# Causal mask of the second layer's first score squares: identity products on TensorE in place of VectorE's additions, with a new written-out order

## What is computed

```python
def _L1_attn_ref(x, w_qkv, w_proj, b_proj):      # B, S, dim = 8, 512, 256; 16 heads of 16
    qkv = (x @ w_qkv).reshape(B, S, 3, heads, head_dim)
    Q, K, V = (qkv[:, :, 0], qkv[:, :, 1], qkv[:, :, 2])
    Q = apply_rope(Q)
    K = apply_rope(K)
    attn = jnp.einsum('bqhd,bkhd->bhqk', Q, K) * scale
    causal = jnp.tril(jnp.ones((S, S), dtype=bool))[None, None]
    attn = jnp.where(causal, attn, jnp.asarray(NEG_INF, attn.dtype))
    attn = jax.nn.softmax(attn, axis=-1)
    out = jnp.einsum('bhqk,bkhd->bqhd', attn, V).reshape(B, S, dim)
    return out @ w_proj + b_proj
```

## Time and profile before

| | us |
|---|---|
| median of 3 runs | 1977.19 |
| lowest, highest | 1975.2, 1977.64 |
| the profiled execution | 1979.78 |
| its span, first to last instruction | 1978.0 |
| PE busy in the span | 1856.4 (94%) |
| DVE busy | 1375.4 (70%) |
| ACT, POOL busy | 907.2, 510.0 |

### The profile page before, as it was taken

The page is one execution under the profiler, slowest core; times in us unless marked ns, Lnnn a source line. Parts: engine busy times, 40 slices in busy tenths (PEclk is TensorE's granted clock), DMA queues, the critical chain, the costliest instruction groups (busy, mean ns, idle before and its releaser), DMA issues.

```text
span 1978.0 us, 39009 instructions
## 1 busy us (share of the span) xinstructions
PE 1856.4 (94%) x15449; PEld 1293.8 (65%) x15449; DVE 1375.4 (70%) x2407; ACT 907.2 (46%) x1116; POOL 510.0 (26%) x597
## 2 busy tenths in 40 slices
...
PEclk8898999999999999888999999999999999999999
...
GB/s 184 58 46 42 59 37 73 50 58 28 86 52 26 40 39 5 171 1 17 44 81 78 54 85 62 65 87 50 75 96 30 86 93 44 86 84 43 112 83 43
DMA packets 171812, 126.26 MB, mean 64 GB/s; under 512 B 113944, under 2 KB 148720, under 8 KB 171248
## 3 DMA queue, kind: packets, MB, share of 16 engines
...
q10 hardware_dynamic: 832, 0.01, 0.0%
...
## 4 chain that ended last, share of the span: by engine, by line
PE 77%; DVE 15%; ACT 4%; issue 3%; POOL 1%; DMA 0%; SPq 0%; DVEq 0%; POOLq 0%; ACTq 0%
PE ps L2041 24%; PE ps L2025 5%; PE ps L1078 5%; PE ps L1922 4%; PE ps L1984 3%; PE ps L983 3%; PE ps L1952 3%; PE ps L2055 2%; PE ps L1108 2%; PE ps L1041 2%; PE ps L1130 2%; PE ps L1023 2%; DVE b_maxima L1689 2%; PE ps L1968 2%; PE ps L1964 2%
## 5 line engine op out<-in xcount | busy, mean ns | idle before, releaser
L2041 PE MATMUL ps<-b_acts,b_hidden_w 128*128 128x512 f32 x2048 | 504.6, 398 | 1.1 <-POOL b_acts L1616 1.1
L2041 PEld LDWEIGHTS ps<-b_acts,b_hidden_w 128*128 128x128 f32 x2048 | 376.2, 188 | 90.9 <-issue 9.8
L452 POOL TENSOR_SCALAR_AFFINE_SELECT a_probs<-a_probs 128x512 f32<-128x512 f32 (+1 forms) x224 | 166.3, 758 | 357.4 <-ACT a_probs L863 249.1
L1608 POOL TENSOR_SCALAR_AFFINE_SELECT b_work<-b_work 128x512 f32<-128x512 f32 x128 | 83.3, 663 | 673.1 <-ACT b_work L1843 673.0
L1879 ACT ACTIVATE b_acts_exact<-ps,c_s 128x512 f32<-128x512 f32 x128 | 88.2, 689 | 297.6 <-PE ps L2041 297.4
L863 ACT ACTIVATE a_probs<-ps 128x2048 f32<-128x2048 f32 (+1 forms) x96 | 153.2, 1595 | 123.5 <-DVEq L713 86.7
L1843 ACT ACTIVATE b_work<-ps 128x2048 f32<-128x2048 f32 (+1 forms) x96 | 153.4, 1597 | 90.8 <-PE ps L1968 89.0
L1689 DVE TENSOR_REDUCE b_maxima<-ps 128x4 f32<-128x2048 f32 (+3 forms) x128 | 187.9, 1489 | 3.3
L1787 DVE CAST b_acts<-b_acts_exact 128x512 fp32r<-128x512 f32 x128 | 55.8, 436 | 164.2 <-ACT b_acts_exact L1879 163.9
L1078 PE MATMUL ps<-a_probs,c_va 128*17 128x192 f32 (+4 forms) x2048 | 136.6, 388 | 2.9 <-issue 1.5
L1686 DVE TENSOR_TENSOR ps<-ps,c_causalr 128x512 f32<-128x512 f32 x128 | 86.1, 696 | 45.2 <-PE ps L1952 43.4
...
## 6 DMA issues: line engine op xcount, KB each, us to landing
b_hidden_w<-turned_h SPq DMA_DIRECT2D x128, 512.0 KB, 3.5
a_raw_next<-in_L_ffn_h_w SPq DMA_DIRECT2D x512, 16.0 KB, 1.8
...
```

The source lines that it names most:

```text
L452: return nc.gpsimd.affine_select(out=z, in_=z, compare_op=ALU.is_ge, fill=0.0, base=0, pattern=[[0, blocks_n], [1, cols]], channel_multipl ...
L2041: ins = nc.tensor.matmul(here, view(hidden_w[:, m, k]), view(src[:, k, i]), start=(k + i == 0), stop=(k == NHID - 1 and i == 1))
```

## The change

For batch 0 of the second layer, `max_fill` issues, after the score products of a fill, four more products for each query tile, one for each head: the 128x128 identity (stationary) by the 128x128 causal triangle, both float32r, accumulated onto the diagonal square. VectorE's additions for batch 0 and the wait for their result go; in their place VectorE waits, at the first part of groups 1 to 3, for the semaphore of its own last write to shift_cols. Batches 1 to 7 keep the additions.

ORDER holds the same 1750 steps. The first 357 stand where they were; between steps 358 and 1697 some 430 have another place among their neighbours, most by 1 to 15 places. The lines around the first pass of the second layer are shown (- before, + after); the other 90 or so are left out.

```diff
@@ ORDER, the lines around the first pass of the second layer @@
...
-1:hT.0 0:kk.6.0 1:proj.0.0 1:proj.0.1 0:wv.31.0 0:wv.31.1 1:proj.0.2 1:proj.0.3 0:kk.6.1 0:lv.30.2 0:lin.31.0 1:tq.0.0 0:lin.31.1 0:wh.31 1:tk.0.0
-0:lh.30 0:lin.31.2 1:max.0.0.0 1:tk.0.1 1:tq.0.1 0:lv.31.0 1:max.0.0.1 0:r.6.0 1:max.0.0.2 1:max.0.1.0 1:again.0.0 0:r.6.1 1:max.0.1.1 0:last.6.0
-0:last.6.1 1:att.0.0.0 1:att.0.0.1 0:flag.0 0:lv.31.1 0:lv.31.2 1:max.0.1.2 0:lh.31 0:turn.7.0 1:values.0.0.0 1:att.0.0.2 1:again.0.1 1:values.0.0.1
-1:tq.0.2 1:att.0.1.0 0:turn.7.1 1:values.0.0.2 1:tk.0.2 1:att.0.1.1 1:max.0.2.0 0:turn.7.2 1:values.0.1.0 0:turn.7.3 1:max.0.2.1 0:out.7.0 1:att.0.1.2
-1:tq.0.3 1:max.0.2.2 1:tk.0.3 1:heads.0.0 1:max.0.3.0 1:again.0.2 1:values.0.1.1 1:values.0.1.2 1:max.0.3.1 0:out.7.1 1:att.0.2.0 1:att.0.2.1
-1:max.0.3.2 1:values.0.2.0 1:values.0.2.1 1:att.0.2.2 1:again.0.3 1:stats.1 0:xT.7.0 1:att.0.3.0 1:heads.0.1 0:xT.7.1 1:values.0.2.2 1:att.0.3.1
-1:values.0.3.0 1:turn.0.0 1:att.0.3.2 1:values.0.3.1 1:values.0.3.2 1:norm.1 1:heads.0.2 1:hT.1 0:kk.7.0 1:heads.0.3 1:proj.1.0 1:turn.0.1 1:proj.1.1
-1:proj.1.2 1:proj.1.3 0:r.7.0 0:kk.7.1 1:ga.0 1:tq.1.0 1:out.0.0 1:tk.1.0 1:max.1.0.0 1:tq.1.1 1:max.1.0.1 1:out.0.1 1:tk.1.1 1:max.1.0.2 0:r.7.1
...
+0:wv.30.0 0:wv.30.1 0:win.31.1 1:stats.1 0:lv.30.2 0:wh.30 1:proj.0.0 1:proj.0.1 0:wv.31.0 1:proj.0.2 0:wv.31.1 1:proj.0.3 0:r.6.0 0:lin.31.0 0:kk.6.0
+1:tq.0.0 0:lin.31.1 0:lv.31.0 0:lh.30 1:tk.0.0 0:lin.31.2 1:max.0.0.0 0:r.6.1 1:tq.0.1 1:max.0.0.1 1:tk.0.1 0:lv.31.1 0:wh.31 1:max.0.0.2 1:max.0.1.0
+0:kk.6.1 1:again.0.0 1:max.0.1.1 0:lv.31.2 0:last.6.0 1:att.0.0.0 0:last.6.1 1:att.0.0.1 0:flag.0 0:lh.31 1:max.0.1.2 0:turn.7.0 1:values.0.0.0
+1:att.0.0.2 1:again.0.1 1:stats.2 1:values.0.0.1 1:att.0.1.0 1:tk.0.2 1:values.0.0.2 1:att.0.1.1 0:turn.7.1 1:values.0.1.0 1:tq.0.2 1:att.0.1.2
+1:max.0.2.0 1:tq.0.3 1:values.0.1.1 0:turn.7.2 1:max.0.2.1 1:tk.0.3 1:values.0.1.2 1:heads.0.0 1:max.0.2.2 0:turn.7.3 1:max.0.3.0 1:again.0.2
+0:out.7.0 1:max.0.3.1 0:out.7.1 1:att.0.2.0 1:att.0.2.1 1:heads.0.1 1:values.0.2.0 1:max.0.3.2 0:xT.7.0 1:values.0.2.1 1:att.0.2.2 1:again.0.3
+0:xT.7.1 1:att.0.3.0 1:values.0.2.2 1:att.0.3.1 1:turn.0.0 1:values.0.3.0 1:att.0.3.2 1:heads.0.2 1:ga.0 1:values.0.3.1 1:values.0.3.2 1:norm.1 1:hT.1
+1:heads.0.3 0:kk.7.0 1:proj.1.0 1:proj.1.1 1:proj.1.2 1:proj.1.3 1:turn.0.1 1:out.0.0 0:r.7.0 1:tk.1.0 1:tq.1.0 0:kk.7.1 1:max.1.0.0 1:tq.1.1
...
@@ -1681,10 +1681,13 @@
         def maximum(b, g, j):
 
             free = arrive(("max", b, g, j))
-            for t, o in MAX_FILLS[j]:
-                square = room["wide"][:, :, o + t * P:o + (t + 1) * P]
-                ins = nc.vector.tensor_tensor(square, square, causal[:, None, :].broadcast_to([P, 4, P]), ALU.add)
-            link(ins)
+            if b == 0 and j == 0 and g:
+                dve.wait_ge(shift_ready, g)
+            if b:
+                for t, o in MAX_FILLS[j]:
+                    square = room["wide"][:, :, o + t * P:o + (t + 1) * P]
+                    ins = nc.vector.tensor_tensor(square, square, causal[:, None, :].broadcast_to([P, 4, P]), ALU.add)
+                link(ins)
             for i, (t, o) in enumerate(MAX_FILLS[j]):
                 ins = nc.vector.tensor_reduce(maxima[:, t, :].unsqueeze(2), room["wide"][:, :, o:o + (t + 1) * P], AX.X, ALU.max, negate=True)
             if j < 2:
@@ -1950,7 +1953,12 @@
                     for part in (qhigh, qlow):
                         for i in range(4):
                             ins = nc.tensor.matmul(here[:, i, o:o + (t + 1) * P], part[rows_of(i), g % 2, t * P:(t + 1) * P],
-                                                   ksplit[rows_of(i), g % 2, 0:(t + 1) * P], start=(part is qhigh), stop=(part is qlow))
+                                                   ksplit[rows_of(i), g % 2, 0:(t + 1) * P], start=(part is qhigh),
+                                                   stop=(part is qlow and b > 0), skip_group_check=(b == 0))
+                if b == 0:
+                    for t, o in MAX_FILLS[j]:
+                        for i in range(4):
+                            ins = nc.tensor.matmul(here[:, i, o + t * P:o + (t + 1) * P], identr[:], causalr[:], start=False, stop=True, skip_group_check=True)
                 ins.then_inc(full_sem, 1)
 
             def scores(step):
```

More of the change, by code:

```diff
@@ L1228 @@
[L1228 to L1231, removed]
@@ L1236 @@
[L1236 to L1239, removed]
@@ L1240 @@
[L1240 to L1243, removed]
@@ L1276 @@
-1:att.2.3.2 1:stats.3 1:values.2.3.0 1:values.2.3.1 1:norm.3 1:h1.1.5.1 1:h1.1.6.0 1:h1.1.6.1 1:values.2.3.2 1:heads.2.2 1:hT.3 1:h1.1.7.0 1:proj.3.0
-1:proj.3.1 1:proj.3.2 1:h1.1.7.1 1:h2.1.0.0 1:proj.3.3 1:h2.1.0.1 1:h2.1.1.0 1:tq.3.0 1:h2.1.1.1 1:tk.3.0 1:h2.1.2.0 1:heads.2.3 1:max.3.0.0
-1:h2.1.2.1 1:h2.1.3.0 1:max.3.0.1 1:h2.1.3.1 1:tk.3.1 1:h2.1.4.0 1:max.3.0.2 1:tq.3.1 1:h2.1.4.1 1:h2.1.5.0 1:again.3.0 1:max.3.1.0 1:h2.1.5.1
-1:h2.1.6.0 1:max.3.1.1 1:turn.2.1 1:h2.1.6.1 1:h2.1.7.0 1:max.3.1.2 1:h2.1.7.1 1:out.2.0 1:att.3.0.0 1:out.2.1 1:last.1.0.0 1:att.3.0.1 1:values.3.0.0
@@ new lines @@
+1:values.2.2.2 1:stats.3 1:h1.1.4.1 1:h1.1.5.0 1:h1.1.5.1 1:heads.2.2 1:att.2.3.2 1:values.2.3.0 1:values.2.3.1 1:h1.1.6.0 1:norm.3 1:hT.3
+1:values.2.3.2 1:h1.1.6.1 1:h1.1.7.0 1:proj.3.0 1:proj.3.1 1:h1.1.7.1 1:proj.3.2 1:h2.1.0.0 1:proj.3.3 1:h2.1.0.1 1:h2.1.1.0 1:tq.3.0 1:h2.1.1.1
+1:tk.3.0 1:h2.1.2.0 1:max.3.0.0 1:h2.1.2.1 1:turn.2.0 1:h2.1.3.0 1:max.3.0.1 1:h2.1.3.1 1:tk.3.1 1:h2.1.4.0 1:tq.3.1 1:max.3.0.2 1:h2.1.4.1 1:h2.1.5.0
+1:max.3.1.0 1:heads.2.3 1:h2.1.5.1 1:h2.1.6.0 1:max.3.1.1 1:turn.2.1 1:h2.1.6.1 1:h2.1.7.0 1:again.3.0 1:max.3.1.2 1:h2.1.7.1 1:out.2.0 1:att.3.0.0
@@ new lines @@
+1:out.2.1 1:last.1.0.0 1:att.3.0.1 1:values.3.0.0 1:last.1.0.1 1:xT.2 1:last.1.1.0 1:att.3.0.2 1:split.2 1:tq.3.2 1:last.1.1.1 1:up.2.0.0 1:tk.3.2
+1:again.3.1 1:max.3.2.0 1:up.2.0.1 1:up.2.1.0 1:values.3.0.1 1:values.3.0.2 1:att.3.1.0 1:up.2.1.1 1:up.2.2.0 1:att.3.1.1 1:up.2.2.1 1:up.2.3.0
+1:max.3.2.1 1:up.2.3.1 1:up.2.4.0 1:values.3.1.0 1:values.3.1.1 1:heads.3.0 1:att.3.1.2 1:max.3.2.2 1:tk.3.3 1:values.3.1.2 1:up.2.4.1 1:again.3.2
+1:up.2.5.0 1:up.2.5.1 1:att.3.2.0 1:heads.3.1 1:up.2.6.0 1:tq.3.3 1:att.3.2.1 1:up.2.6.1 1:up.2.7.0 1:values.3.2.0 1:max.3.3.0 1:values.3.2.1
@@ new lines @@
+1:up.2.7.1 1:h1.2.0.0 1:max.3.3.1 1:turn.3.0 1:h1.2.0.1 1:h1.2.1.0 1:max.3.3.2 1:h1.2.1.1 1:h1.2.2.0 1:att.3.2.2 1:again.3.3 1:h1.2.2.1 1:h1.2.3.0
+1:stats.4 1:values.3.2.2 1:att.3.3.0 1:h1.2.3.1 1:h1.2.4.0 1:att.3.3.1 1:values.3.3.0 1:h1.2.4.1 1:h1.2.5.0 1:att.3.3.2 1:values.3.3.1 1:norm.4
+1:h1.2.5.1 1:heads.3.2 1:hT.4 1:values.3.3.2 1:h1.2.6.0 1:proj.4.0 1:proj.4.1 1:h1.2.6.1 1:proj.4.2 1:h1.2.7.0 1:proj.4.3 1:h1.2.7.1 1:h2.2.0.0
+1:tq.4.0 1:h2.2.0.1 1:tk.4.0 1:h2.2.1.0 1:tk.4.1 1:max.4.0.0 1:h2.2.1.1 1:tq.4.1 1:ga.3 1:h2.2.2.0 1:max.4.0.1 1:h2.2.2.1 1:heads.3.3 1:h2.2.3.0
```

166 lines of the change are left out of this document (85 added, 81 removed).

## The result

| | us |
|---|---|
| before, median of 4 runs | 1977.24 (1975.2 to 1977.64) |
| after, median of 4 runs | 1962.8 (1957.98 to 1964.61) |
| ratio after to before | 0.9918 [0.99, 0.9936] |
| the profiled execution of after | 1963.62, its span 1961.9 |

The kernel got faster by 14.4 us, 0.8%.

The account below looks back on a forecast made before the run. The prediction took the seam at 740 to 960 us, no engine full, as bound by a chain of waits between PE, DVE and ACT through the room "wide". 0 - 2.5 - 1.9 = -4.4 us gave 1972.8 us, range 1966 to 1982.

Parts of the forecast that it names:

- the seam: 740 to 960 us, first layer's last steps and second's first pass: PE idle 44.8 of 220 us, clock 0.87.
- Part A: Batch 0's mask, second layer: 7.0 us of products on the chain against 6.6 us of additions removed, taken as zero.
- Part B: Moves followed singly around the second layer's first pass: value steps lv.31.1 and lv.31.2 ahead of flag, -2.5 us.
- The trade of places of r.6.x and kk.6.x: r.6.1 and kk.6.1 trade places, both a PE step with an ACT or DVE tail: priced at nothing.
- stats and ga: stats.1 and stats.2 moved, the latter hidden by DVE idle time; ga.0, a POOL addition, moved earlier: no cost counted.
- xT at nothing: xT.7.1 moved ahead of att.0.3.0: no gain, since norm.1 also needs value products that waited for POOL.
- Part C: The other moves, about 400 in both layers, not followed singly: one common stall less, -1.9 us, ends -8 and +4.
- The sum: 0 - 2.5 - 1.9 = -4.4 us, median forecast 1972.8 us; the case of 1970 to 1976 had chance 0.44.
- the clock recovers: Rival, chance 0.17: with fewer holes in the seam PE holds the higher clock, -5 us beyond the sum, 1968 us.

Follow-up runs that it names:

- e1_mask_only: Kernel before with its old ORDER but the new mask code (identity products instead of VectorE's additions for batch 0): 1982.53 us, ratio 1.0002 to before.
- e5: Kernel before with the mask code and only lv.31.1 moved ahead of max.0.0.2 and lv.31.2 ahead of last.6.0: 1982.64 us, ratio 1.0009.
- e6: Kernel before with the mask code and only the new places of r.6.0, r.6.1, kk.6.0 and kk.6.1: 1987.89 us, ratio 1.004.
- e13: The whole change, but xT.7.0 and xT.7.1 put back behind again.0.3 and att.0.3.0: 1963.85 us, ratio 0.9920 to before.
- c_order_only: Kernel before with the new ORDER but the old mask code (VectorE's additions kept): 1969.82 us, ratio 0.9942.
- e7: Kernel before with the mask code and only steps 784 to 812 put among themselves as in the new order: 1983.29 us, ratio 1.0014.
- e8: Kernel before with the mask code and only steps 680 to 783 put among themselves as in the new order: 1981.11 us, ratio 1.0000.
- e14: Kernel before with the mask code and only steps 358 to 679 of the first layer in the new order: 1981.78 us, ratio 1.0008.

## Why the prediction had the direction and not the size

**What bounds it** was read rightly in the main: the seam, with its idle PE time and its low clock. Between L736 and norm.1 stand 9.9 of the 16 us of the two profiled executions; 3.8 are ahead of it and 2.4 behind.

**Part A, the mask at zero.** Its prices hold: 0.50 and 0.92 us a set, and e1_mask_only is at 1.0002. Its count does not: the forecast put 11 of the 16 sets on the chain. The chain of waits after, 770 to 850 us, by line:

```profile
by line: DVE b_maxima L1692 15.6%; PE ps L1961 11.8%; PE ps L1108 11.2%; ACT b_work L1846 10.7%; PE ps L1955 10.6%; PE ps L1992 7.0%; PE ps L1976 6.0%; PE ps L1972 5.4%; PE ps L1130 4.8%; issue 4.0%; PE ps L1941 1.8%; PE ps L1088 1.3%; PE p
```

L1961 has 11.8% of 80 us, 9.4 us. The pieces of the chain, too, list all twelve fills with their 64 products. By that count the trade should have come out near +3 (9.4 - 6.6), and in the new order it came out at -6. It did so because neither term is what the sum had: PE's busy time rose by 3.3 us and not by 10.3, as the other products ran at a higher clock, and its idle time fell by 9.9 where the additions were put at 6.6.

**Part B, -2.5.** Zero alone (e5): the first ten us of its pass ran at full speed, where e1 shows 0.83, but the clock fell later, to 0.83 in the second ten and 0.72 in the third, and the pass is as long as e1's. The trade of places of r.6.x and kk.6.x, at nothing, was +7.5 alone (e6), the largest single miss. stats and ga have no run of their own; xT at nothing holds (e13).

**Part C, -1.9.** The idle time outside the seam fell by 2.3 us, as written. But the order alone brings 11.5 us (0.58% of 1980, c_order_only). That is the term that was mis-sized: B + C at -4.4 against -11.5. In its profiled execution, against that of before, some 4 us of it stand ahead of L736, 3 between there and norm.1 and 2 behind; the forecast gave the seam B's 2.5 and all the rest 1.9. None of it is in the pass itself (74.2 us against 71.0), and the 3 are PE's busy time (102.7 against 106.0), with the same 27.9 us idle: not one stall less, as the forecast had it, but a clock of 0.88 in place of 0.86.

**The step that failed** is "The sum": 0 - 2.5 - 1.9, terms read one by one from the old order and added. B + C measured -11.5 in place of -4.4, and A, nothing in the old order, -6 in the new. A was added up with a fixed mean clock of 0.82 and a fixed share of waits, as if both were properties of the stretch; they are results of the order. The rival that says so for the clock, "the clock recovers", had 0.17, and its -5 beyond the sum, 1968, is still 5 us above the result. The argument against it, that the reductions of 23.5 us stay and the holes with them, was wrong at its last words: the reductions stayed, 23.5 us after as before, but PE's idle time in the pass fell from 17.5 us (71.0 - 53.6) to 9.9 (67.8 - 57.9). The sign written down for it, a clock above 0.87 by 0.04 or more in 740 to 960, came out at 0.92. That e1_mask_only is level with before looks like the forecast's zero for A, but in its profiled execution the stretch from L736 to norm.1 is 4.2 us longer than before, with 15 of the 16 sets on its chain of waits; the agreement is in part luck.

**What stays open.** Which single moves fill the holes; e6, e7 and e8 say only that it takes both sides of step 784. Some 4 us of the gain stand ahead of L736 in all executions with the full new order (728.4 to 731.1 us, ten kernels, against 731.0 to 738.3 in nine with the old first layer), yet e14, with the new first layer up to step 679, has no gain in its time, and its L736 starts at 733.1. Where that part comes from isn't known. The 3 us between the last maxima and norm.1 I put down to values.0.2.0: before, 24 value products of 3.62 us at half speed stood between that fill and att.0.2.2 on PE, and after one third of them goes ahead of it. That is argued from the two timelines and was not isolated; the clock went from 0.85 to 1.00 in the same interval, and e13 gives 1.5 of the 3 us back, so it is one share among others.
